# Raw rows and centred keys in the first attention, and gate logits with the tokens standing, in a two-layer Flamingo kernel on one Trainium2 core

## The reference

```
x = x + tanh(g_xattn[0]) * L0_xattn(layernorm(x), ctx, ctx, mask)
x = x + tanh(g_ffn[0])  * L0_ffn(layernorm(x), ...)

L0_xattn: scores = hidden @ keys^T ; where(mask == 0, -1e10) ; softmax over the 77 keys ; @ values
L0_ffn:   logits = x @ gate_w^T + gate_b   (8 experts)
          the 2 best experts of each token, weighted by the softmax, plus a shared expert of 512
          expert: (silu(x w1 + b1) * (x w3 + b3)) w2 + b2
```

## Time and profile before

| | us |
|---|---|
| median of 3 runs | 687.16 |
| lowest, highest | 682.91, 690.23 |
| the profiled execution | 684.5 |
| its span, first to last instruction | 682.8 |

### The profile page before, as it was taken

One profiled execution on the slowest core, in us unless ns is written; L12 is line 12 of the kernel. 1 busy time (PEld: TensorE's weight loads), 2 busy tenths in 40 slices (PEclk: granted clock), 3 DMA queues, 4 the chain that ended last, 5 costly groups with the idle time before them and its releaser, 6 DMA issues.

```text
span 682.8 us, 12771 instructions
## 1 busy us (share of the span) xinstructions
PE 622.5 (91%) x3602; PEld 511.8 (75%) x3602; DVE 440.6 (65%) x1291; ACT 376.7 (55%) x836; POOL 251.0 (37%) x340
## 2 busy tenths in 40 slices
PE   6789999879988999999999998899679969999997
PEld 5577887667766788888888876677567847877886
DVE  4577787865753666666666645638737766775755
ACT  3678988767622555555555542345534654673633
POOL 4125555564351335322332237761460453100100
PEclk8889999999998999999999999999879999999999
DMA  5435545573065933333333328620130232000000
GB/s 164 131 108 169 158 164 168 193 236 132 29 250 176 297 107 109 103 104 107 103 108 102 100 67 283 233 77 1 32 93 32 64 113 72 2 30 32 31 32 32
DMA packets 58628, 77.53 MB, mean 114 GB/s; under 512 B 7543, under 2 KB 47682, under 8 KB 58306
## 3 DMA queue, kind: packets, MB, share of 16 engines
q1 hardware_dynamic: 51218, 57.57, 26.3%
q0 software_dynamic: 7344, 19.14, 8.6%
HBM read 44.52 MB, written 32.17 MB: 112 GB/s over the span
## 4 chain that ended last, share of the span: by engine, by line
PE 62%; DVE 13%; issue 10%; ACT 6%; DMA 3%; SPq 2%; another core or an unknown queue 2%; POOL 1%; ACTq 0%; DVEq 0%; POOLq 0%
PE bank L1078 12%; PE bank L1080 11%; PE bank L1079 11%; PE bank L1427 3%; PE bank L1428 3%; PE bank L1448 3%; PE bank L1449 3%; PE bank L1283 2%; PE bank L1292 2%; PE bank L1040 2%; DVE st L1825 2%; PE bank L1390 2%; PE bank L1064 1%; DMA xg<-rows_by_expert 1%
## 5 line engine op out<-in xcount | busy, mean ns | idle before, releaser
L546 POOL TENSOR_TENSOR yg<-yg,b 128x256 f32<-128x256 f32 x71 | 52.3, 736 | 120.2 <-ACT yg L643 120.2
L1777 DVE TENSOR_TENSOR hb<-bank,b 128x512 f32<-128x512 f32 x71 | 49.1, 692 | 60.5 <-PE bank L1080 60.1
L1427 PE MATMUL bank<-n4Th,wint 128*128 128x512 f32 x192 | 79.7, 415 | 6.7 <-DVE n4Tl L1888 3.1
L506 POOL DMA_INDIRECT rows_by_expert<-n,pos x64 | 65.0, 1016 | 55.1 <-DVE pos L1661 38.7
L1428 PE MATMUL bank<-n4Tl,wint 128*128 128x512 f32 x192 | 77.2, 402 | 0.0
L643 ACT ACTIVATE hTh<-bank 128x256 fp32r<-128x256 f32 x71 | 27.4, 386 | 82.9 <-PE bank L1292 82.9
L588 POOL DMA_INDIRECT yr<-expert_out,out_row x64 | 65.2, 1019 | 21.6 <-issue 18.6
L643 ACT ACTIVATE g3h<-sl 128x512 fp32r<-128x512 f32 x60 | 37.8, 630 | 45.5 <-DVE sl L1894 28.5
L1080 PE MATMUL bank<-w13h,xTl 128*128 x142 | 56.6, 399 | 0.0
L1079 PE MATMUL bank<-w13l,xTh 128*128 x142 | 56.3, 396 | 0.0
L1078 PE MATMUL bank<-w13h,xTh 128*128 x142 | 56.0, 394 | 0.2 <-DVE xTl L1784 0.2
(11 more groups left out here) (258 smaller groups left out, 1828.2 us busy)
## 6 DMA issues: line engine op xcount, KB each, us to landing
xg<-rows_by_expert SPq DMA_DIRECT2D x71, 128.0 KB, 2.0
expert_out<-yg SPq DMA_DIRECT2D x71, 128.0 KB, 1.7
stage<-in_wexp SPq DMA_DIRECT2D x24, 256.0 KB
xin<-in_x SPq DMA_DIRECT2D x8, 512.0 KB, 4.5
x_shared<-x SPq DMA_DIRECT2D x8, 512.0 KB
xa<-x_shared SPq DMA_DIRECT2D x4, 1024.0 KB
out<-ost SPq DMA_DIRECT2D x8, 512.0 KB, 2.9
wint<-in_wint POOLq DMA_DIRECT2D x3, 768.0 KB, 7.9
```

The lines of the kernel that those rows point to most:

```text
L506: pool.indirect_dma_start(out=xs, out_offset=bass.IndirectOffsetOnAxis(ap=pos[p][:, k, j:j + 1], axis=0), in_=n2[p][:, j, :], in_offset=No ...
L546: pool.tensor_tensor(yg[s], yg[s], b2[:, bass.ds(e, 1), :].rearrange("p a d -> p (a d)"), ALU.add)\
L1427: mm(o, s, n4Th[c][:, k, :], start=(k == 0), stop=False)
L1777: tt(hb[p], bank[:, p, :], b13[:, bass.ds(e, 1), :].rearrange("p a n -> p (a n)"), ALU.add)\
```

## The change

In the attention, layernorm(x)·key is rstd · x·(key - mean(key)). So the rows are no longer normalised before the scores: `t1` turns the raw rows of `xin`, the keys are centred once (`ctxC`, two products of `ctxT` with a matrix of 1/256, then two subtractions on DVE), and the reciprocal deviation comes in at the softmax (`scale`) and on the row maximum. `ln1_apply` and POOL's shift for it are gone. NEG becomes -1e30.

In the gate the turned rows stand (128x128, one tile) and the weights move: 16 columns (high and low part side by side, `gw2`) for the rows' high part, 8 for their low part, so 16 products for each group. The result already has the tokens on the partitions; `logit_copy` and `gate_back` are gone, and `route_a` has one more addition.

In the prologue the order changes: `t1(0)` and `t1_copy(0)` come first, `keep_warm` is spread, the last three slices of `wsh` and their low parts move into step 0 (on ACT after `pt_copy(0)`, on DVE after `ln2_stats(0)`, both ahead of `expert_high(0,0)` and `expert_low(0,0)`), `ln1_stats(1)` moves behind `row_max(0)`, and the nine small operations on the shared bias move into step 0 behind `expert_low(0,0)`.

```diff
 # POOL
+            chained(pool.memset(mean_of, 1.0 / D))
-            def rstd_of(which, g, applied):
+            def rstd_first(g):
+                pool.wait_ge(sem("stats0"), g + 1)
...
+                pool.tensor_scalar(ve[0], mv[0][:, :, 1], EPS, None, ALU.add).then_inc(sem("var0"), 1)
...
+                pool.tensor_tensor(rstd1[g % 2], ve[0], halfpow[:, 0:GT], ALU.pow).then_inc(sem("rstd0"), 1)
+            def rstd_second(g):
...
 # ACT
-            def ln1_apply(g, p, tiles=range(GT)):
...
                     act.activation(probs[:, j, :], bank[:, 6, j * P:j * P + KV], ACT.Exp, bias=negmax[:, j:j + 1],
-                                   accum_out=psums[:, j:j + 1]).then_inc(sem("probs_done"), 1)
+                                   scale=rstd1[g % 2][:, j:j + 1], accum_out=psums[:, j:j + 1]).then_inc(sem("probs_done"), 1)
-            def logit_copy(f):
...
                 pt_copy(g)
-                if nxt:
-                    ln1_apply(g + 1, 1 - p, first)
+                if not ffn:
+                    for c in range(3):
+                        stage_high(c, wsh[:, 3 + c, :], 2)
...
-            for c in range(3):
+            t1_copy(0)
+            for c in range(2):
                 stage_high(c, wsh[:, c, :], 1)
-            ln1_apply(0, 0)
-            t1_copy(0)
             act.wait_ge(sem("mask_ready"), 1)
             scores_copy(0)
+            stage_high(2, wsh[:, 2, :], 1)
...
-            for c in range(3):
-                stage_high(c, wsh[:, 3 + c, :], 2)
             softmax(0)
 # PE
             def t1(g, rows_in):
-                pe.wait_ge(sem("n1_done"), GT * (g + 1))
+                pe.wait_ge(sem(f"x_in{g % 2}"), 16 * (g // 2 + 1))
...
             def gate(g):
...
-                for k in range(KD):
-                    last = three(bank[0:NE, 7, :], gwh[:, k, :], gwl[:, k, :], n2Th[:, k, :], n2Tl[:, k, :], k == 0, k == KD - 1)
-                last.then_inc(sem("gateT_done"), 1)
-            def gate_back(f):
...
+                    t = slice(j * P, (j + 1) * P)
+                    both, first = bank[:, 7, j * 2 * NE:(j + 1) * 2 * NE], bank[:, 7, j * 2 * NE:j * 2 * NE + NE]
+                    for k in range(KD):
+                        mm(both, n2Th[:, k, t], gw2[:, k, :], start=(k == 0), stop=False, skip_group_check=True)
+                        last = mm(first, n2Tl[:, k, t], gwh[:, k, :], start=False, stop=(k == KD - 1), skip_group_check=True)
                 last.then_inc(sem("gate_done"), 1)
...
             pe.wait_ge(sem("pool_const"), 2)
-            keep_warm(24)
-            pe.wait_ge(sem("pool_const"), 16)
-            t1(0, n1)
-            pe.wait_ge(sem("ctx_in"), 32)
+            keep_warm(16)
+            pe.wait_ge(sem("pool_const"), 17)
+            t1(0, xin[0])
+            pe.wait_ge(sem("ctx_in"), 16)
+            for k in range(KD):
+                last = mm(bank[:, 6, 0:B * KV], mean_of, ctxT[:, :, k, :], start=(k == 0), stop=(k == KD - 1))
+            last.then_inc(sem("ctx_mean"), 1)
+            keep_warm(12)
+            pe.wait_ge(sem("ctx_centred"), KD)
             scores(0, 0)
+            keep_warm(10)
             scores_back(0)
-            keep_warm(5)
+            keep_warm(8)
 # DVE
-                dve.tensor_reduce(negmax, s, AX.X, ALU.max, negate=True).then_inc(sem("negmax_done"), 1)
+                dve.tensor_reduce(negmax, s, AX.X, ALU.max, negate=True).then_inc(sem("rowmax_done"), 1)
+                dve.wait_ge(sem("rowmax_done"), g + 1)
+                dve.wait_ge(sem("rstd0"), g + 1)
+                tt(negmax, negmax, rstd1[g % 2], ALU.mult).then_inc(sem("negmax_done"), 1)
...
+                else:
+                    for c in range(3):
+                        low_part(c, wsh[:, 3 + c, :], wsl[:, 3 + c, :], 2)
                 expert_low(g, 0)
+                if setup:
+                    setup()
```

More of the change, by code:

```diff
@@ L137, in flamingo_kernel @@
         ve = [w1.put(f"ve{p}", [P, GT], F32) for p in range(2)]
[L138 to L141, removed]
+        rstd1 = [w1.put(f"rstd1{p}", [P, GT], F32) for p in range(2)]
+        rstd2 = w1.put("rstd2", [P, GT], F32)
+        negm = w1.put("negm", [P, GT], F32)
+        nb2 = w1.put("nb2", [P, GT], F32)
         logit = w1.put("logit", [P, GT, NE], F32)
@@ L156, in flamingo_kernel @@
         w0 = Area(area_b2, top)
-        w0.put("raw_pad", [P, GT * D * 4], F32)
+        w0.put("raw_pad", [P, GT * D * 7], F32)
         bs2f = w0.put("bs2f", [3, D], F32)
@@ L654, in expert_high @@
                 stage_high(c, high, g + 3)
[L656 to L660, removed]
-            def ln1_apply(g, p, tiles=range(GT)):
-                if g:
-                    act.wait_ge(sem("t1_done"), KD * g)
-                normal(g, 0, n1, xin[p], "n1_done", tiles)
             def ln2_apply(g, p, tiles=range(GT)):
@@ L669, in ln2_apply @@
                     act.wait_ge(sem(f"scattered{p}"), g // 2 * (2 * GT * 16))
-                normal(g, 1, n2[p], x1[p], "n2_done", tiles)
+                act.wait_ge(sem("shift1"), g + 1)
+                for j in tiles:
+                    act.activation(n2[p][:, j, :], x1[p][:, j, :], ACT.Identity, bias=nb2[:, j:j + 1],
+                                   scale=rstd2[:, j:j + 1]).then_inc(sem("n2_done"), 1)
             def t1_copy(g):
@@ L778, in step @@
                 if ffn:
-                    logit_copy(f)
                     silu(f, 2)
@@ L870, in norm @@
             def norm(which, u, src, dst, done, tiles):
-                act.wait_ge(sem(f"shift{which}"), NG + u + 1)
+                act.wait_ge(sem(f"shift{which}"), which * NG + u + 1)
                 for j in tiles:
@@ L1039, in scores @@
                 for k in range(KD):
-                    last = mm(bank[0:KV, 6, :], ctxT[:, b, k, :], n1T[:, k, :], start=(k == 0), stop=(k == KD - 1))
+                    last = mm(bank[0:KV, 6, :], ctxC[:, k, b, :], n1T[:, k, :], start=(k == 0), stop=(k == KD - 1))
                 last.then_inc(sem("s_done"), 1)
@@ L1201, in step @@
                     up(f, 2)
-                    gate_back(f)
                 if nxt:
-                    t1(g + 1, n1)
+                    t1(g + 1, xin[1 - p])
                 if ffn:
@@ L1664, in route_d, with step @@
                     .then_inc(sem("route_kept"), 1)
-            def step(g, p, ffn=True, nxt=True, more=True):
+            def step(g, p, ffn=True, nxt=True, more=True, setup=None):
                 f = g - 1
@@ L1727, in _, with shared_bias @@
             dve.memset(rank_base, 0.0).then_inc(sem("base_done"), 1)
-            row_max(0)
-            for c in range(3):
-                low_part(c, wsh[:, 3 + c, :], wsl[:, 3 + c, :], 2)
-            step(0, 0, ffn=False)
+            def shared_bias():
+                for c in range(3):
+                    chained(cp(part[c], bs2f))
+                    if c < 2:
+                        chained(tt(bs2f, bs2f, part[c], ALU.subtract))
+                chained(ts(pick, part[0], row_of[:, 0:1], None, ALU.mult))
+                chained(stt(pick, part[1], row_of[:, 1:2], pick, ALU.mult, ALU.add))
+                stt(bs2, part[2], row_of[:, 2:3], pick, ALU.mult, ALU.add).then_inc(sem("bias_ready"), 1)
+            step(0, 0, ffn=False, setup=shared_bias)
             for g in range(1, NG):
```

90 lines of the change are left out of this document (46 added, 44 removed).

## The result

| | before | changed |
|---|---|---|
| median of 18 runs each, us | 686.45 | 689.68 |
| lowest, highest, us | 682.91, 692.28 | 682.91, 699.16 |
| ratio, 95% interval | | 1.0054, 1.0029 to 1.008 |
| the profiled execution, its span, us | 684.5, 682.8 | 687.69, 686.0 |
| mean granted clock of that execution | 0.962 | 0.960 |

The forecast was 679.7 (671 to 687). The changed kernel is 0.5% slower instead, outside the range, though within the 1% that was called no change. Ratios leave out runs more than 1.5% above the fastest run of their kernel, so a ratio need not be the quotient of two medians: here three of the changed kernel's 18 runs go, and in the first four experiments 18 of the 35 of the kernel before.

The account below looks back on a forecast made before the run. PE was taken to bound stage 1's step 2, with stalls at the expert stage and a long prologue chain. 1.5 + 4.4 + 1.6 + 0 = 7.5 us off 684.5 gave 677.0, or 679.7 as median, range 671 to 687.

Parts of the forecast that it names:

- Part 1: Gate in PE-bound steps of stage 1: 0.25 us gained in each of six steps, 1.5 us, bounds 0 and 6.
- the products' own time: Gate: 16 narrow products at 0.115 us each, 1.85 us, replacing 2.0 us of products and back-turn.
- Rival (c): Gate: narrow products do not pipeline, 0.30 us each, 4.8 instead of 2.0 us; median near 701; chance 0.08.
- PE gains 0.15 us a step, at most 1.0: Gate in PE-bound steps: PE's gain from products of 1.85 us replacing 2.0 us; ACT's relief adds 0.1.
- Part 2: Expert-stage stall, steps 5 and 6: PE stops waiting for the logits, the stall moves to scores; 4.4 us gained, bounds 2.7 and 6.
- Nothing else is then late: Expert stage, steps 5 and 6: once scores start earlier, nothing else delays; second layer norm's row norm follows on ACT as before.
- Part 3: Prologue and step 0: expert reload takes back 4.1 us, first up about unchanged, half the clock's worth gained: 1.6 us, bounds -2 and +5.
- Part 4: Tail of stage 1: gate(7) costs the same, route_a(7)'s remote wait of 3.2 us stays; 0 us, bounds -2 and +3.
- Rival (a): Reload and clock take the time: first up 1 us later and cold, g = 6 scores cold; median near 684; 0.27 with (d), scores also awaiting the stage.

Follow-up runs that it names:

- the first four experiments: Four follow-ups on one chip: old gate in changed kernel 1.001; new gate in kernel before 1.0041; 128 moving gate columns 0.9951; unread 384-column products between narrow ones 1.0023.
- The wide gate: Changed kernel with 128 instead of 16 or 8 moving columns in the gate's 16 products: 679.81 us, ratio 0.9951; on later chips 0.9933 and 0.9897.
- the attention part alone: Changed kernel with the gate of before, its logits copy and back-turns: 684.45 us, ratio 1.001; on a later chip 665.42 us, 0.9968.
- the gate part alone: Kernel before with the 16 narrow gate products, without logits copy and back-turn: 688.6 us, ratio 1.0041.
- the version with the late copy: Changed kernel, narrow gate, with step 0's first expert copy behind group 1's scores copy on ACT and its low part behind the row maximum on DVE: 688.71 us, 1.0069.

## Why the prediction was wrong, point by point

In the profiled executions the span grew by 3.2 us, where 7.5 less was forecast. Up to the end of step 1 it is 2.1 us shorter (forecast 1.6), in steps 2 to 4 it is 4.0 longer, in steps 5 and 6 2.5 shorter (forecast 4.4), in step 7 4.5 longer, from there to stage 2 1.9 shorter (forecast 0), and in stages 2 and 3 1.2 longer. So the miss is mainly in steps 2 to 4 and 7, which are Part 1.

- **Part 1, the products' own time: right.** 16 x 0.112 = 1.79 us, against 1.85 forecast. By the rule for the load in the Trainium skill, page "TensorE: Matmul & The Clock Gate", section "LDWEIGHTS (loading the stationary operand)", the estimate was 1.7 (0.107 each); the trace agrees, with 0.112 us a product. Rival (c), products that do not pipeline, has the right side and the wrong mechanism.
- **Part 1, "PE gains 0.15 us a step, at most 1.0", with bounds of 0 and 6 for the six steps: this is the step that failed.** It priced what the products take and not what they do to the clock of the work behind them. In the changed kernel steps 3, 4 and 7 are 3.0, 1.0 and 4.5 us longer. The wide gate, with equal product times, starts stage 2 7.9 us earlier (213.65 against 221.58, on another chip), and in the medians on one chip it is worth 2.8 and 4.7 us. The gain of 1.5 less these 2.8 to 7.9 makes a term of -1.3 to -6.4 us. Of the three, step 7's share is the least sure: a wait stood ahead of its fall, and the attention part alone, with the old gate, has a step 7 of 25.6 us, 1.7 longer than before.
- **Part 2, the stall at the expert stage: right in kind, about half in size.** PE no longer waits for the logits (it does so 3.8 us in the attention part alone), and waits 1.0 us for `n1T` at g = 6 and not at all at g = 5, where 1 to 3 us each were forecast. Steps 5 and 6 together are 2.5 us shorter, not 4.4. The load landed at 127.73 and at 153.37, the second 2.4 us later than the 150.96 that the sum held fixed, and a fall of the clock lies in each of the two steps. "Nothing else is then late" was too easy; how the missing 1.9 us divide between the load and the clock is open.
- **Part 3, the prologue: right.** `t1(0)` at 7.25 (forecast 7.3), scores at 11.85 (11.8), `residual1(0)` at 21.37 (21.0), the stage's load issued at 25.24 (24.9) and landed at 27.70 (27.1 to 28.4), first `up` at 37.82 (36 to 38). The scores of group 1 ran at half clock, 3.70 us with their tail. The clock at the first `up`, given half its worth, came in full: with 34.57 for `t2(0)`, 0.65 later than before, step 1 is 2.8 us shorter: 2.1 us net against 1.6.
- **Part 4, the tail: near.** The remote wait is 3.2 us again; from `t2(7)` to stage 2 it is 1.9 us shorter, against 0.
- **The rivals.** Rival (a) named the clock, but only behind waits; its price was a median near 684. Its two signs did not come: the first `up` and the scores of g = 6 ran at full clock. None had a fall in a stretch that PE fills. The sign that the prediction set for being wrong, steps g = 2 to 4 longer than 20 us each, did come: 20.3, 23.0 and 21.2 us.
- **The size.** On two later chips the same kernel has ratios of 0.9985 and 0.9976. The 0.5% more of the first measurement is not a property of the kernel alone. That the narrow products cost time beside wide ones came out on both chips where the two were run together.

## What to carry to other kernels

When a change makes products narrow, price not only their own time but the clock of what comes behind them: read the granted clock over stretches where PE is busy throughout, and not just over its waits. Where products of few moving columns start no closer together than wide ones do (here 0.11 us with 16 and with 128), more moving columns cost nothing, so widening them is a cheap test and here the cure. A gain ahead of a fixed load, such as the expert's weights in step 6, can be lost at that load; look there first. And compare such variants on one chip over several runs, for a single profile can be of the fastest of them.

## What was not expected of the hardware

- The granted clock fell to 1.2 GHz within products that follow each other without a gap: at 84.3 us in the changed kernel, at 66.2 in the gate part alone, and not with 128 moving columns in the same products. What in the chip answers to the columns is not shown. The Trainium skill, page "TensorE: Matmul & The Clock Gate", section "HAM oscillation — how this bites in real kernels", puts such falls down to waits of PE between bursts. The window of 84 to 91.5 with PE busy 7.50 of 7.50 us and nothing waiting ahead of it shows another cause.
- It did not happen behind every gate. In the changed kernel steps 1 and 2 have the same 16 products at the same pace and no fall on any of the three chips' profiles, though the version with the late copy has one behind the gate of step 1 (43.5 to 47.5); why is open.
- Other narrow products may do the same. In the version with 64 columns the clock fell at 78.5 us, behind eight products of one column. This is its timeline of PE, 0.23 us and then 0.18 to 0.22 from start to start; it was seen once and not tested, and in the kernel before the same eight products have no fall behind them.

```profile
77.80 0.65 PE L1170 MATMUL bank<-bqk,kT 16*77 16x1 f32 x8
78.63 0.40 PE L1074 MATMUL bank<-n2Th,wsh 128*128 128x256 f32 x1 [0.19 <-DVE x L1604]
78.86 0.39 PE L1075 MATMUL bank<-n2Tl,wsh 128*128 128x256 f32 x1
79.04 0.42 PE L1076 MATMUL bank<-n2Th,wsl 128*128 128x256 f32 x1
```
